# Attention of the second layer: transposing in two 64-row halves, in another order

## The reference, cut to what matters

```python
q, k, v = jnp.einsum('bsx,xMnd->Mbnsd', x, qkv)
a = jnp.einsum('bnsd,bntd->bnst', q, k) * q.shape[-1] ** (-0.5)
cum = jnp.cumsum(rpe_bias[:, :s], axis=-1)
rel = jnp.arange(s)[:, None] - jnp.arange(s)[None, :]
bias = jnp.where(rel >= 0, cum[:, jnp.clip(rel, 0)], PAD)
a = jax.nn.softmax(a + bias, axis=-1)
mix = jnp.einsum('bnst,bntd->bnsd', a, v)
return jnp.einsum('bnsd,ndx->bsx', mix, out_w)
```

## Time and profile before

| | us |
|---|---|
| median of three runs | 2612.39 |
| the runs | 2607.81 to 2614.0 |
| span of the profiled execution | 2604.6 |
| TensorE products busy | 2306.1 (89%) |
| VectorE busy | 1723.5 (66%) |
| ScalarE busy | 1323.7 (51%) |
| GpSimd busy | 924.0 (35%) |

### The profile page before, as it was taken

The page is one execution under the profiler, slowest core; times in us unless marked ns, Lnnn a source line. Parts: engine busy times, 40 slices in busy tenths (PEclk is TensorE's granted clock), DMA queues, the critical chain, the costliest instruction groups (busy, mean ns, idle before and its releaser), DMA issues. The chain is left out here.

```text
span 2604.6 us, 48558 instructions
## 1 busy us (share of the span) xinstructions
PE 2306.1 (89%) x16540; PEld 1370.8 (53%) x16540; DVE 1723.5 (66%) x5002; ACT 1323.7 (51%) x2685; POOL 924.0 (35%) x1132
## 2 busy tenths in 40 slices
PE   5489999998999999999999478799999997789886
PEld 2357667995666667766667365422222223333333
DVE  7646664763666555565555756588888882678896
ACT  2146665554665666665666523156666665423222
POOL 2046665663567633332333314011111110035453
PEclk8689999997999999999999779689999998889998
DMA  6311113113011100000000007111111100000000
GB/s 160 106 54 32 31 32 80 47 34 126 17 33 17 28 2 18 2 18 3 1 2 2 3 18 226 56 21 34 33 39 40 34 19 3 34 0 0 9 8 16
DMA packets 77916, 93.70 MB, mean 36 GB/s; under 512 B 10145, under 2 KB 56242, under 8 KB 76002
## 3 DMA queue, kind: packets, MB, share of 16 engines
q1 hardware_dynamic: 64178, 77.23, 9.9%
q0 software_dynamic: 13488, 13.28, 2.6%
HBM read 54.55 MB, written 35.53 MB: 35 GB/s over the span
## 5 line engine op out<-in xcount | busy, mean ns | idle before, releaser
L978 ACT ACTIVATE WA<-a_E 128x1024 f32<-128x1024 f32 (+3 forms) x384 | 300.6, 815 | 158.8 <-PE a_E L917 112.5
L634 ACT COPY a1b_PT<-a1b_T 128x512 f32<-128x512 f32 (+3 forms) x288 | 153.5, 533 | 206.0 <-PE a1b_T L545 206.0
L455 POOL TENSOR_SCALAR XR<-XR,a1b_rinv 128x384 f32<-128x384 f32 (+1 forms) x192 | 161.5, 853 | 268.8 <-DVE a1b_rinv L707 268.4
L535 PE MATMUL a1b_S<-a1b_Kf,a1b_Qf 64*128 64x512 f32 (+3 forms) x1164 | 243.0, 522 | 0.0
L702 DVE COPY a1b_PT<-a1b_T 128x128 f32<-128x128 f32 (+3 forms) x288 | 140.6, 488 | 154.0 <-PE a1b_T L545 154.0
L560 PE MATMUL a1b_O<-a1b_PT,WA 128*64 128x128 f32 x3456 | 225.8, 277 | 14.8 <-ACT WA L638 14.8
L893 PE MATMUL a_S<-a_KS,a_QS 54*128 54x512 bf16 (+3 forms) x768 | 204.2, 352 | 33.6 <-DVE a_mx L1014 20.1
L560 PEld LDWEIGHTS a1b_O<-a1b_PT,WA 128*64 128x64 f32 x3456 | 186.0, 137 | 81.8 <-ACT a1b_PT L634 39.7
L455 POOL TENSOR_SCALAR WA<-WA,a1b_rinv 128x128 f32<-128x128 f32 (+1 forms) x194 | 121.1, 636 | 215.1 <-DVE a1b_rinv L707 215.1
L893 PEld LDWEIGHTS a_S<-a_KS,a_QS 54*128 54x128 bf16 x768 | 60.4, 93 | 235.8 <-DVE a_mx L1014 127.7
L625 ACT ACTIVATE XR<-XR,a1b_nmax 128x384 f32<-128x384 f32 (+1 forms) x192 | 168.1, 881 | 3.1
(11 more groups left out here) (433 smaller groups left out, 5140.7 us busy)
## 6 DMA issues: line engine op xcount, KB each, us to landing
WA<-in_w SPq DMA_DIRECT2D x8, 1024.0 KB, 9.0
a_QS<-qstack SPq DMA_DIRECT2D x32, 216.0 KB
a_KS<-kstack SPq DMA_DIRECT2D x32, 216.0 KB
a1b_tb<-tab SPq DMA_DIRECT2D x12, 512.0 KB
qstack<-f_parts SPq DMA_DIRECT2D x24, 256.0 KB
kstack<-f_parts SPq DMA_DIRECT2D x24, 256.0 KB
f_slots<-f1r_zrows SPq DMA_DIRECT2D x9, 516.0 KB, 6.2
f1t_xs<-f_slots SPq DMA_DIRECT2D x9, 516.0 KB, 5.1
```

What stands on the lines that cost most here:

```text
L455: pool.tensor_scalar(soft(i0, u), soft(i0, u), rinv[:, n:n + 1], 1.0, ALU.mult, ALU.mult).then_inc(n_sb, 1)
L535: pe.matmul(pS[k % NB][:, 0:hi - lo], Qf[half, b0 % 2, i0 * P:(i0 + 1) * P], Kf[half, b0 % 2, lo:hi], start=True, stop=True).then_inc(s_ps, 1)
L634: act.copy(PT[:, i % 2 * HG + u, lo:hi], pT[0][:, 0:hi - lo]).then_inc(t_sb_a, 1)
L978: act.activation(PT[:, q % NP, :, off:CH], pE[q % 2][:, :, off:CH], ACT.Exp).then_inc(e_sb, 1)
```

## The change

- A turn of a head does for each block j two transposes of 64 rows (the upper and lower half of the query rows), the upper half into bank `pT[0]`, the lower into `pT[1]`, 64 columns each. One semaphore increment marks the end of a whole turn, not of a chunk.
- Every turn fills both banks, so it first waits until ScalarE and VectorE have both copied the turn before it. `PT` gets the shape blocks x halves x 64; ScalarE copies the upper halves of all blocks of a turn in one instruction, VectorE the lower halves. `values` reads the same 128 columns of a block as before.
- The projection of a block moves in front of its two turns. Behind turn (i, 0) come the scores of chunk 0, behind turn (i, 1) those of chunk 1, then the values.
- ScalarE and VectorE follow that order: the reader of the projection comes first, and on VectorE the bias of chunk 0 stands between copies (i, 0) and copies (i, 1). The reciprocals stay behind copies (i, 0).

```diff
-    PT = ph.sb("PT", [P, 4, T])
+    PT = ph.sb("PT", [P, 4, TT, 2, QH])
...
             def turn(it, i, u):
-                pe.wait_ge(n_sb, it * U + i * HG + u + 1)
-                for c in range(i // CT + 1):
-                    k = turn_at[i, u, c]
-                    pe.wait_ge((t_sb_a, t_sb_d)[k % 2], it * HALF + k // 2 + 1)
-                    lo, hi = span(i, c)
-                    for j in range(lo // P, hi // P):
-                        ins = pe.transpose(pT[k % 2][:, j * P - lo:(j + 1) * P - lo], soft(i, u)[:, j * P:(j + 1) * P],
-                                           G["ident"][:, :])
-                    ins.then_inc(t_ps, 1)
+                n = it * U + (i * HG + u)
+                pe.wait_ge(n_sb, n + 1)
+                pe.wait_ge(t_sb_a, n + 1)
+                pe.wait_ge(t_sb_d, n + 1)
+                pe.sem_inc(passed_pe, 1)
+                for j in range(i + 1):
+                    for h in range(2):
+                        rows = slice(h * QH, (h + 1) * QH)
+                        ins = pe.transpose(pT[h][:, j * QH:(j + 1) * QH], soft(i, u)[rows, j * P:(j + 1) * P],
+                                           G["ident"][rows, rows])
+                ins.then_inc(t_ps, 1)
 
             def values(it, s, i):
-                done = turn_at[i, HG - 1, i // CT] + 1
-                pe.wait_ge(t_sb_a, it * HALF + (done + 1) // 2 + 1)
-                pe.wait_ge(t_sb_d, it * HALF + done // 2 + 1)
+                done = it * U + (i + 1) * HG
+                pe.wait_ge(t_sb_a, done + 1)
+                pe.wait_ge(t_sb_d, done + 1)
...
                         ins = pe.matmul(pO[half, i % CT * P:(i % CT + 1) * P], V[s][:, j, half],
-                                        PT[:, i % 2 * HG + u, j * P:(j + 1) * P], start=(j == 0), stop=(j == i))
+                                        PT[:, i % 2 * HG + u, j, :, :].rearrange("p h q -> p (h q)"),
+                                        start=(j == 0), stop=(j == i))
...
                 for i in range(TT):
-                    turn(it, i, 0)
                     if i in PROJECT:
...
                         output(it, s, OUT[i])
-                    turn(it, i, 1)
-                    for c in range(2):
-                        scores(it, b, i + LEAD, c)
+                    for u in range(HG):
+                        turn(it, i, u)
+                        scores(it, b, i + LEAD, u)
                     if i >= 1:
                         values(it, s, i - 1)
...
             def copies(it, i, u):
-                for c in range(i // CT + 1):
-                    k = turn_at[i, u, c]
-                    if k % 2 == 0:
-                        lo, hi = span(i, c)
-                        act.wait_ge(t_ps, it * R + k + 1)
-                        act.copy(PT[:, i % 2 * HG + u, lo:hi], pT[0][:, 0:hi - lo]).then_inc(t_sb_a, 1)
+                act.wait_ge(t_ps, it * U + (i * HG + u + 1))
+                act.copy(PT[:, i % 2 * HG + u, 0:i + 1, 0, :], pT[0][:, 0:(i + 1) * QH].rearrange("p (j q) -> p j q", q=QH))\
+                   .then_inc(t_sb_a, 1)
...
                 for i in range(TT):
-                    copies(it, i, 0)
                     if PROJECT.get(i) in (2, 3):
                         project_k(it + 1, 1 - s, PROJECT[i] - 2)
                     if PROJECT.get(i) in (4, 5):
                         project_v(it + 1, 1 - s, PROJECT[i] - 4)
+                    copies(it, i, 0)
                     copies(it, i, 1)
...
             def copies(it, i, u):
-                for c in range(i // CT + 1):
-                    k = turn_at[i, u, c]
-                    if k % 2:
-                        lo, hi = span(i, c)
-                        dve.wait_ge(t_ps, it * R + k + 1)
-                        dve.tensor_copy(PT[:, i % 2 * HG + u, lo:hi], pT[1][:, 0:hi - lo]).then_inc(t_sb_d, 1)
+                dve.wait_ge(t_ps, it * U + (i * HG + u + 1))
+                dve.tensor_copy(PT[:, i % 2 * HG + u, 0:i + 1, 1, :], pT[1][:, 0:(i + 1) * QH].rearrange("p (j q) -> p j q", q=QH))\
+                   .then_inc(t_sb_d, 1)
...
                 for i in range(TT):
-                    copies(it, i, 0)
-                    inverse(it, i + 1)
                     if i in OUT:
                         add(it, (b - 1) % B, OUT[i])
                     if PROJECT.get(i) in (0, 1):
                         project_q(it + 1, 1 - s, PROJECT[i])
-                    copies(it, i, 1)
-                    for c in range(2):
-                        bias(g2, gp, b, i + LEAD, c)
+                    for u in range(HG):
+                        copies(it, i, u)
+                        if u == 0:
+                            inverse(it, i + 1)
+                        bias(g2, gp, b, i + LEAD, u)
```

More of the change, by code:

```diff
@@ L366, in attention @@
     chunks = [(i, c, u) for i in range(TT) for c in range(i // CT + 1) for u in range(HG)]
-    turns = [(i, u, c) for i in range(TT) for u in range(HG) for c in range(i // CT + 1)]
     R = len(chunks)
     chunk_at = {key: k for k, key in enumerate(chunks)}
-    turn_at = {key: k for k, key in enumerate(turns)}
-    HALF = R // 2
+    QH = P // 2
     NB = 4
@@ L391, in attention @@
     s_ps, s_sb, p_sb, r_inv, n_sb = (ph.sem(n) for n in ("sps", "ssb", "psb", "rinvs", "nsb"))
-    passed_dve, passed_pool = ph.sem("passeddve"), ph.sem("passedpool")
+    passed_dve, passed_pool, passed_pe = ph.sem("passeddve"), ph.sem("passedpool"), ph.sem("passedpe")
     t_ps, t_sb_a, t_sb_d, pv_ps, o_sb, y_ps, x_sb = (
```

## The result

The changed kernel takes 2672.99 us (median of 4 runs, 2666.66 to 2679.57) against 2610.1 us before: a ratio of 1.0246, 95% interval 1.023 to 1.0261. It is 2.5% slower. I had forecast 2612 us and no change. The time is inside my range (2555 to 2690), but the sum behind it was short by some 60 us. The profiled execution has a span of 2677.6 us, 73 more than the one of before; it is the slowest of the four, so the runs say 63.

The account below looks back on a forecast made before the run. TensorE, busy 98%, was taken as the bound: per iteration 3.38 us gained against 3.45 us of new waits, +0.07, times 32 is +2 us, given back by the openings: 2612 us, no change; range 2555 to 2690.

Parts of the forecast that it names:

- The pair of half products: Each transpose as two 64-row products: 0.062 us a pair, gaining 72 x 0.047 = 3.38 us an iteration.
- Rivals 1 and 4: 1: pair at 0.11 to 0.12, no overlap, 2724 us, chance 0.14; 4: sequencer limits pairs to 0.085, 2665 us, chance 0.07.
- The waits: New TensorE waits for copies and the output bank: 3.45 us an iteration, against 3.38 gained.
- Turn (5,1): TensorE's wait before row 5's second turn, for copies behind the output addition: 0.83 us.
- Turn (7,1): TensorE's wait before row 7's second turn, for a copy against short scores: 0.44 us.
- Turn (1,0): TensorE's wait before row 1's first turn, for VectorE's copy (0,1) queued behind two bias passes: 0.58 us.
- The output bank: Row 5: wait before the values, with the emptying behind ScalarE's copy (5,1): 1.21 us against 0.66, 0.55 more.
- a clock that I left at 0.99: Granted TensorE clock in the attention stretches, 0.99, the 2.4 GHz level; everything was costed as TensorE time.
- The changes of shape. Cost nothing: Array shape changes on TensorE: three per row both times, same three kinds of exposed load in another order, so no cost.
- one of my signs of being wrong: Wrong if the pair's step is near 0.11, waits at i=5 to 7 are missing, or scores start late behind a turn.
- rival 3: Switching between transposing and plain products inside the 64-row shape costs 0.15 us, 24 or so times: 2727 us, chance 0.05.
- Both have 40% idle, so this load alone costs nothing: ScalarE and VectorE make 16 copies each per iteration, up from 12; VectorE's +1.5 us was costed at nothing.

Follow-up runs that it names:

- before_late_empty: Kernel before, with ScalarE emptying the output bank only after the first of the two exponentials of step i=5: 2666.92 us, ratio 1.0228.
- after_early_empty: Changed kernel, with ScalarE emptying the output bank at the start of step i=5, before copies (5,0): 2595.42 us, ratio 0.9955.
- bank_wait_alone: Changed kernel with copy (0,1) before row 0's bias, and rows 5 to 7's projection between chunk 0 scores and turn (i,1); emptying behind copy (5,1): 2577.23 us.
- halves_old_order: Changed kernel's half transposes into both banks, but in the order of before (turn, projection, turn, scores, values) on all three engines: 2628.68 us, ratio 1.0091.

## Why the prediction was wrong

**The pair of half products: right.** I took 0.062 us. In the trace after, eight half products fill 0.46 us and twelve 0.59; less the last one's record (0.22) and the first load (0.06) that leaves 0.18 for three steps and 0.31 for five, 0.060 and 0.062 a pair. Right after a wait, sixteen fill 0.71: less 0.22 and the 0.03 of the load still open, 0.46 for seven steps, 0.066. Rivals 1 and 4 fall. The rule of the Trainium skill's page "TensorE: Matmul & The Clock Gate", Part 3, The mechanism, that a load overlaps a running product only in another row group, does not hold in this trace: at 0.061 load (0.06) and stream (0.053) overlap within a half. (The same section also lets a load into the background weight buffer be pulled ahead, which would fit; no run here can tell.)

**The waits: right in place, nearly in size.** An idle time is listed from the modelled end of the product before, 0.17 us after its last column, to a start some 0.03 before the next one's first column, so 0.20 is added to compare with my terms. Turn (5,1): 0.65 in nearly all iterations, as in the one at 1364.84 (the 0.74 of the one at 1022.69 is the exception), so 0.85, forecast 0.83. Turn (7,1): 0.48, forecast 0.44. Turn (1,0): mostly 0.56 + 0.20 less the 0.15 of the change of shape, 0.61, forecast 0.58. The output bank: 1.15 + 0.20 - 0.15 = 1.20, forecast 1.21.

**The step that failed: a wait was taken at its length.** My sum took the 0.83 and 1.21 us of row 5 only as time lost, under a clock that I left at 0.99. Idle time in that place also lowered the clock behind it, and the values of row 4 and the projection of row 6 ran at half speed: 1.4 us for each of 27 low stretches, 38 us. I named no rival with that mechanism. before_late_empty and after_early_empty show it in both directions; bank_wait_alone makes it likely that it takes both waits. The Trainium skill's page "TensorE: Matmul & The Clock Gate", section HAM oscillation — how this bites in real kernels, says that idle gaps between bursts of products bring back the low clock and make the products after them slow. The traces agree in kind: the four microseconds behind the two waits have a clock of 0.57. The gaps here are shorter than the waits for transfers in that section's example: 0.65 and 1.15 us, with one turn between them.

**A term that was missed: "The changes of shape. Cost nothing".** I counted loads in the open only where the shape changes. But a full load of 0.107 us for the scores also stands right behind a transpose that streams only 0.053. The loads in the trace after:

```profile
1011.99 0.33 PEld L545 LDWEIGHTS a1b_T<-ident,XR 64*128 64x128 f32 x8 [0.76 <-issue]
1012.23 0.31 PEld L533 LDWEIGHTS a1b_S<-a1b_Kf,a1b_Qf 64*128 64x128 f32 x4
```

The scores' first load starts with the last transpose at 1012.23 us. The scores end at 1012.29 + 1.08, and less 0.17 of latency and 0.853 of columns their first column comes at 1012.35, while the transpose's last column passed at 1012.28. So 0.05 to 0.07 is open, 12 times an iteration: about 0.65 us, 21 us in all. This is read from the trace and not tested by itself. It is one of my signs of being wrong, scores that start late behind a turn, and rival 3 had the place right, a switch inside the 64-row shape, but with 0.15 us, 24 times. It nearly closes the account: my sum for an iteration without the output bank's wait was 35.1 - 1.2 = 33.9; with 0.65 here, and some 0.1 for the waits that came out longer, it is about 34.7, and after_early_empty has 34.8 to 35.1. The rest, 0.1 to 0.4, is open.

**Cover by an idle engine.** "Both have 40% idle, so this load alone costs nothing" was true for the changed order. It would have been wrong in the old one, as halves_old_order shows: there VectorE's copies were late by 1.7 us an iteration.

**The sum with the terms mended.** Without the fall of the clock the period is 36.25 us, 1.2 more than before: 39 us in 32 iterations, where I had 2. The fall adds 38. Together 77; the iteration with the loop's jump back takes 1.8 us less than that, the openings of the two parts some 7.6 less, and the program after the last values 5.2 us more: 73, as the profiled pair differs; the medians differ by 63. The 5.2 us lie behind the changed part (1147.3 us against 1142.2; the eleven traces have 1140.2 to 1147.3), so they may be a matter of the single execution, which is the longest of its four by 4 us and 6.6 above their median. That is not shown.

## What to carry to other kernels

When a change puts waits on a TensorE that had hardly any, price each wait twice: at its length, and again for the half-speed stretch that may follow if it is long (1.74 us here) or if two come close together (0.65 and 1.15). Look at the granted clock by stage before and after, and compare the same rows in iterations with and without the fall. If two buffers that were used in turn become one, the place of the emptying in its engine's queue counts, not that engine's idle share; and a long independent piece of work, here the projection, belongs between the two users. Then the faster products paid (2535.67 us), while one moved instruction was worth 28 us even without them (2581.13).

## What the runs showed of the hardware that was not expected

Waits far shorter than an iteration can lower the clock, and not each time: with one wait of 1.74 us in row 5 it fell in 16 of 29 periods of the same program, with 1.15 us in none, with 0.62 us in none, and with waits listed as 0.65 and 1.15 us close together in 26 of 29. The cost was 1.4 to 1.6 us each time. The length of the wait does not settle it alone: iterations with and without a fall have the same waits, and in before_late_empty they mostly alternate three by three. What does is not shown.

TensorE keeps the two 64-row halves apart far enough that scores of one head started while three transposes of the other half were still to come.
